# Late routed rows in 22 whole tiles and 5 tiles shared by two experts, with column-strip matmuls and a load for each half

## The reference, cut to what matters

```python
scores = softmax(x @ gate_w.T); topk_ids, topk_w = grouped_topk(scores)      # 2 experts for each row
combine = zeros((T, 8)).at[arange(T)[:, None], topk_ids].add(topk_w)
gu = einsum('th,eih->tei', x, w13_weight)            # w13: 8 x 1024 x 256
gate, up = gu[..., :512], gu[..., 512:]
act = silu(gate) * up * combine[:, :, None]
out = einsum('tei,ehi->th', act, w2_weight)          # w2: 8 x 256 x 512
x = x + out
```

## Time and profile before

| | |
|---|---|
| median of 3 runs | 552.11 us |
| span of the profiled execution, first to last instruction | 551.1 us |
| that execution's time with what lies around the span | not given; the median is 1.0 us above the span |
| busy: PE / PEld / DVE / ACT / POOL | 98 / 81 / 52 / 46 / 31% of the span |
| granted TensorE clock | 0.999 of full |
| moved by DMA | 74.30 MB, mean 135 GB/s |

### The profile page before, as it was taken

How to read it: one execution, slowest core, us unless ns; L and a number is a source line. 1 busy time by engine, 2 the same in 40 slices (tenths; PEclk the granted TensorE clock), 3 DMA queues, 4 the chain that set the end, 5 groups by cost and what they waited for, 6 DMA issues and landing times.

```text
span 551.1 us, 11061 instructions
## 1 busy us (share of the span) xinstructions
PE 538.4 (98%) x3967; PEld 444.4 (81%) x3968; DVE 284.0 (52%) x847; ACT 254.1 (46%) x587; POOL 168.7 (31%) x152
## 2 busy tenths in 40 slices
PE   9999999999999999999999889999999999999995
PEld 7887878777655676777777679999999999999995
DVE  4867676988562776855788865722212111212110
ACT  1343476263346767687787834542222222222221
POOL 2211000002145222332222043354335454445533
PEclk9999999999999999999999999999999999999999
DMA  8940000000110000300470657968788888898733
GB/s 320 403 141 1 2 0 2 0 1 2 38 39 0 2 2 1 116 1 2 135 287 7 227 172 244 318 187 268 221 246 219 248 229 236 239 255 238 239 66 38
DMA packets 28651, 74.30 MB, mean 135 GB/s; under 512 B 5600, under 2 KB 20320, under 8 KB 23360
## 3 DMA queue, kind: packets, MB, share of 16 engines
q1 hardware_dynamic: 18592, 61.87, 31.9%
q0 software_dynamic: 7488, 10.39, 10.6%
q10 hardware_dynamic: 2528, 1.48, 0.9%
HBM read 62.88 MB, written 10.85 MB: 134 GB/s over the span
## 4 chain that ended last, share of the span: by engine, by line
PE 93%; ACT 4%; DVE 1%; issue 1%; POOL 0%; DVEq 0%; POOLq 0%
PE ps L897 64%; PE ps L1193 12%; PE ps L901 11%; ACT ring L617 2%; PE ps L1041 1%; PE ps L1050 1%; ACT ring L624 1%; PE ps L1053 1%; PE ps L1044 1%; PE ps L981 1%; PE ps L1024 1%; ACT HF L629 0%; ACT ring L658 0%; POOL out_x L422 0%; PE ps L1122 0%
## 5 line engine op out<-in xcount | busy, mean ns | idle before, releaser
L897 PE MATMUL ps<-keep,arena 128*128 128x128 f32 (+2 forms) x976 | 114.9, 274 | 0.0
L897 PEld LDWEIGHTS ps<-keep,arena 128*128 128x128 f32 x976 | 112.8, 192 | 1.5 <-issue 1.1
L2014 DVE TENSOR_TENSOR keep<-keep,ps 128x512 f32<-128x512 f32 x39 | 26.8, 686 | 145.7 <-PE ps L897 124.2
L422 POOL DMA_INDIRECT out_x<-arena,row_no x38 | 59.9, 1576 | 102.1 <-DMA out_x<-arena,row_no 65.2
L1193 PE MATMUL ps<-arena,keep 128*128 x312 | 73.7, 380 | 0.1
L665 ACT COPY keep<-ps 128x256 f32<-128x256 f32 x39 | 14.5, 372 | 107.1 <-PE ps L901 103.8
L381 POOL TENSOR_TENSOR ring<-arena,keep 128x512 f32<-128x512 f32 x32 | 33.5, 1049 | 96.9 <-PE ps L897 79.8
L1193 PEld LDWEIGHTS ps<-arena,keep 128*128 128x128 f32 x312 | 56.4, 190 | 6.6 <-issue 0.3
L617 ACT ACTIVATE ring<-ps,mx 128x128 f32<-128x128 f32 x192 | 52.3, 403 | 6.2 <-DVE mx L1714 6.2
L897 PE MATMUL ps<-ring,arena 128*32 128x128 f32 (+1 forms) x640 | 53.1, 348 | 1.5 <-ACT ring L624 1.4
L373 POOL TENSOR_TENSOR var_x<-var_x,minus_half 128x4 f32<-128x4 f32 x16 | 16.5, 1036 | 115.8 <-DVE var_x L1570 115.8
(11 more groups left out here) (266 smaller groups left out, 816.2 us busy)
## 6 DMA issues: line engine op xcount, KB each, us to landing
arena<-in_w SPq DMA_DIRECT2D x29, 1024.0 KB
w_first<-in_w SPq DMA_DIRECT2D x10, 1024.0 KB
arena<-in_w SPq DMA_DIRECT2D x8, 512.0 KB, 7.3
keep<-in_keep SPq DMA_DIRECT2D x1, 3115.0 KB, 20.8
ring<-in_fold SPq DMA_DIRECT2D x1, 2112.0 KB, 12.7
arena<-in_x SPq DMA_DIRECT2D x4, 512.0 KB, 10.5
arena<-in_ctxT SPq DMA_DIRECT2D x4, 512.0 KB, 7.1
arena<-in_ctx SPq DMA_DIRECT2D x4, 384.0 KB, 11.2
```

Source lines behind the costliest of these rows:

```text
L422: pool.indirect_dma_start(out=out_d, out_offset=bass.IndirectOffsetOnAxis(ap=rows_at, axis=0), in_=YO[t % DEEP], in_offset=None, compute_o ...
L897: ins = pe.matmul(out, w, m, start=(k == 0), stop=(k == len(pairs) - 1))
L2014: dve.tensor_tensor(HA[r % 2], HA[r % 2], ps[:, 2 * (r % 2) + 1, :], ALU.mult).then_inc(act_ok, 1)
```

## The change

`NT` falls from 39 to 36: 9 early tiles, 22 late whole tiles of one expert, and 5 shared ones at t = 15, 19, 23, 27 and 31 (`SPLIT_AT`), each made of two halves of 64 pairs, which may belong to different experts. Expert by expert, full tiles (and rests above 64) go to whole tiles while there are any, the rest goes to halves.

A shared tile differs from a whole one at each station. SP loads two w13 (one for each half) into two buffers of their own, `W13_HALF`, in the arena. POOL gathers its 128 rows as before, but adds them by two DMAs of 64 rows, the second of which waits until the first has landed (a row can be in both halves). PE forms gate and up with the rows standing and the weights moving (`gate_up_halves`, 8 matmuls of 64 standing and 512 moving columns, the two halves in the two column strips of the array); the product then has the pairs on partitions, so it is turned by 4 transposes (`turn_act`) and copied by ACT (`act_turned`) before `down_halves` (8 matmuls of 64 x 256). ACT copies the two experts' w2 into `W2_HALF` three tiles ahead (two copies of 128 x 1024). The loops are written out, with no `Fori`.

On DVE the places of the whole tiles are found and published first (`late_tiles`, `late_hot(0, ...)`, `late_rows`), those of the halves after it (`late_halves`, `half_tiles`, `late_hot(1, ...)`, `half_rows`) between the steps of tiles 7 to 9, and PE has a second `place_late(1)`, again 32 small matmuls, ahead of tile 9's step.

```diff
-NT = B * S * NPICK // P + NE - 1
 EB = 2 * GB
 EARLY = -(-(EB * S * NPICK - NE * (P - 1)) // P)
-LATE = NT - EARLY
+HALF = P // 2
+LEFT = B * S * NPICK - EARLY * P
+HALVES = LEFT // HALF + NE - 1
+LATE = HALVES // 2 - NE // 2
+SHARED = -(-HALVES // 2) - LATE
+WHOLE, STRIPS, PLACES = EARLY + LATE, 2 * SHARED, LATE + 2 * SHARED
+NT = WHOLE + SHARED
+SPLIT_AT = tuple(NT - 5 - 4 * n for n in reversed(range(SHARED)))
...
+            def weights(c, to, landed):
+                e = sp.value_load(e_id[0:1, c:c + 1], min_val=0, max_val=NE - 1)
+                sp.dma_start(to, w13_d[bass.ds(e, 1), :, :].rearrange("e p n -> (e p) n")).then_inc(landed, 16)
+
+            def weights_of_half(n, h):
+                if n:
+                    sp.wait_ge((u_ps, y_ps)[h], SPLIT_AT[n - 1] + 1)
+                else:
+                    sp.wait_ge(e_known, 3)
+                    sp.wait_ge(stored[NG - 1], 32)
+                    sp.wait_ge(s["gl_ps"], NG)
+                    sp.wait_ge(s["ot_ps"], ALL)
+                weights(WHOLE + 2 * n + h, W13_HALF[h], half_in)
...
             sp.wait_ge(e_known, 1)
-            for t in range(NT):
-                if t == 1:
+            ran = [t for t in range(NT) if t not in SPLIT_AT]
+            for c, t in enumerate(ran):
+                if c == 1:
                     sp.wait_ge(s["ot_ps"], 2 * UNITS)
-                if t == 2:
+                if c == 2:
                     sp.wait_ge(s["ot_ps"], 3 * UNITS)
                     sp.wait_ge(xi_in[1], 16)
-                if t == 3:
+                if c == 3:
                     sp.wait_ge(stored[2], 32)
-                if t == EARLY:
+                if c == EARLY:
                     sp.wait_ge(e_known, 2)
-                if t >= DEEP:
-                    sp.wait_ge(u_ps, t - DEEP + 1)
-                e = sp.value_load(e_id[0:1, t:t + 1], min_val=0, max_val=NE - 1)
-                sp.dma_start(W13[t % DEEP], w13_d[bass.ds(e, 1), :, :].rearrange("e p n -> (e p) n")).then_inc(w13_in[t % DEEP], 16)
-            sp.wait_ge(added, 16 * NT)
+                if c >= DEEP:
+                    sp.wait_ge(u_ps, ran[c - DEEP] + 1)
+                weights(c, W13[c % DEEP], w13_in[c % DEEP])
+                for n in range(SHARED):
+                    for h in range(2):
+                        if t == SPLIT_AT[n] + (1 + h if n else 2 * h - 1):
+                            weights_of_half(n, h)
+            sp.wait_ge(added, 16 * adds_up_to(NT - 1))
...
+                    pool.wait_ge(added, 16 * adds_up_to(min(t, NT - 2) - 1))
+                c = column(t)
+                if t in SPLIT_AT:
+                    for n in range(2):
+                        own = slice(HALF * n, HALF * (n + 1))
+                        rows_at = row_upper[:, c - WHOLE:c - WHOLE + 1] if n else row_no[0:HALF, c:c + 1]
+                        if n:
+                            pool.wait_ge(added, 16 * (adds_up_to(t) - 1))
+                        pool.indirect_dma_start(out=out_d, out_offset=bass.IndirectOffsetOnAxis(ap=rows_at, axis=0),
+                                                in_=YO[t % DEEP][own, :], in_offset=None, compute_op=ALU.add).then_inc(added, 16)
+                    return
...
+            def w2_of_halves(n):
+
+                if n:
+                    act.wait_ge(y_ps, SPLIT_AT[n - 1] + 1)
+                else:
+                    act.wait_ge(e_known, 3)
+                    act.wait_ge(w2_in, 16 * NE)
+                    act.wait_ge(s["ot_ps"], ALL)
+                for h in range(2):
+                    c = WHOLE + 2 * n + h
+                    e = act.value_load(e_id[0:1, c:c + 1], min_val=0, max_val=NE - 1)
+                    act.copy(W2_HALF[h], w2e[:, bass.ds(e * W2_N, W2_N)]).then_inc(w2_half, 1)
+
+            def act_turned(r):
+                act.wait_ge(at_ps, split_up_to(r))
+                act.copy(HA[r % 2], bank(FEED)).then_inc(at_ok, 1)
+
+            def step(r):
+                turned(r + 2)
+                answer(r - 1)
+                if r in SPLIT_AT:
+                    act_turned(r)
+                gate(r + 1)
+                if r + 3 in SPLIT_AT:
+                    w2_of_halves(SPLIT_AT.index(r + 3))
...
+            def gate_up_halves(r):
+
+                pe.wait_ge(xt, r + 1)
+                pe.wait_ge(half_in, 32 * split_up_to(r))
+                for g in range(2):
+                    for k in range(KD):
+                        for h in range(2):
+                            own = slice(HALF * h, HALF * (h + 1))
+                            at = (2 * k + g) * INTER
+                            ins = pe.matmul(ps[own, 2 * (r % 2) + g, :], XIT[r % 2][:, k, own], W13_HALF[h][:, at:at + INTER], start=(k == 0), stop=(k == KD - 1))
+                    ins.then_inc((g_ps, u_ps)[g], 1)
+
+            def turn_act(r):
+                pe.wait_ge(act_ok, r + 1)
+                if r == SPLIT_AT[0]:
+                    pe.wait_ge(pair_known, 1)
+                    pe.wait_ge(routed, 3)
+                for i in range(INTER // P):
+                    ins = turn(bank(FEED)[:, i * P:(i + 1) * P], HA[r % 2][:, i * P:(i + 1) * P])
+                ins.then_inc(at_ps, 1)
+
+            def down_halves(r):
+                pe.wait_ge(at_ok, split_up_to(r))
+                pe.wait_ge(w2_half, 2 * split_up_to(r))
+                pe.wait_ge(y_ok, r - 1)
+                for i in range(INTER // P):
+                    for h in range(2):
+                        own = slice(HALF * h, HALF * (h + 1))
+                        ins = pe.matmul(Y_PS[r % 2][own, :], HA[r % 2][:, i * P + HALF * h:i * P + HALF * (h + 1)], W2_HALF[h][:, i * D:(i + 1) * D],
+                                        start=(i == 0), stop=(i == INTER // P - 1))
+                ins.then_inc(y_ps, 1)
+
+            def step(r):
+                turn_in(r + 2)
+                if r in SPLIT_AT:
+                    turn_act(r)
+                if r + 1 in SPLIT_AT:
+                    gate_up_halves(r + 1)
+                else:
+                    gate_up(r + 1)
+                if r in SPLIT_AT:
+                    down_halves(r)
+                else:
+                    down(r)
...
-            turn_pair()
-            tiles_of(pe, step)
-            gate_up(0, NT - 1)
-            down(0, NT - 2)
-            down(0, NT - 1)
+            gate_up(4, (0,))
+            gate_up(4, (1,))
+            turn_in(6)
+            down(3)
+            down(4)
+            gate_up(5, (0,))
+            gate_up(5, (1,))
+            gate_up(6, (0,))
+            place_late(0)
+            turn_in(7)
+            down(5)
+            gate_up(6, (1,))
+            gate_up(7, (0,))
+            turn_in(8)
+            down(6)
+            gate_up(7, (1,))
+            gate_up(8, (0,))
+            gate_up(8, (1,))
+            turn_in(9)
+            down(7)
+            gate_up(9, (0,))
+            gate_up(9, (1,))
+            turn_in(10)
+            down(8)
+
+            place_late(1)
+            for r in range(EARLY, NT - 2):
+                if r == EARLY + 1:
+                    turn_pair()
+                step(r)
+            gate_up(NT - 1)
+            down(NT - 2)
+            down(NT - 1)
...
             late_tiles()
-            late_hot()
-            gated(0, 5)
-            pick(0, 6)
+            late_hot(0, whole_at[:, :])
+            gated(5)
+            pick(6)
             late_rows()
             last_rows()
-            gated(0, 6)
-            pick(0, 7)
-            gated(0, 7)
-            pick(0, 8)
-            gated(0, 8)
-            pick(0, 9)
-            pick(0, 10)
-            gated(0, 9)
-            match_rows()
-            tiles_of(dve, step)
-            gated(0, NT - 1)
+            gated(6)
+            pick(7)
+            late_halves()
+            gated(7)
+            pick(8)
+            half_tiles()
+            gated(8)
+            pick(9)
+            late_hot(1, tile_at)
+            pick(10)
+            gated(9)
+            half_rows()
+            for r in range(EARLY, NT - 2):
+                step(r)
+                if r == EARLY + 1:
+                    match_rows()
+            gated(NT - 1)
             add_matched()
```

More of the change, by code:

```diff
@@ L268, in build, with split_up_to, column, adds_up_to @@
         XT_PS, Y_PS = ps[:, 4, 0:D], [ps[:, 5 + u, 0:D] for u in range(2)]
[L270 to L279 removed]
+        assert SPLIT_AT[0] > EARLY + 2
+        def split_up_to(r):
+            return sum(t <= r for t in SPLIT_AT)
+        def column(r):
+            return WHOLE + split_up_to(r) - 1 if r in SPLIT_AT else r - split_up_to(r)
+        def adds_up_to(r):
+            return r + 1 + split_up_to(r)
         def bank(k):
@@ L1504, in _ @@
             hidden1(15)
-            turn_in(0, 0)
-            turn_in(0, 1)
-            gate_up(0, 0, (0,))
+            turn_in(0)
+            turn_in(1)
+            gate_up(0, (0,))
             outputs1(15)
-            gate_up(0, 0, (1,))
```

(28 more changed lines are left out.)

396 lines of the change are left out of this document (227 added, 169 removed).

## The result

| | before | after |
|---|---|---|
| time, median (lowest to highest) | 551.93 us (551.71 to 552.84) | 570.08 us (563.59 to 572.95, 4 runs) |
| ratio after / before | | 1.028 (95%: 1.024 to 1.032) |
| profiled execution: time, span | | 563.59, 560.6 us |
| add(15) starts, add(NT-2) starts | 429.82, 544.83 us | 432.16, 554.38 us |

Forecast were 549.9 us and a range of 543 to 560. The change makes the kernel 2.8% slower.

The account below looks back on a forecast made before the run. The adds' chain, not PE, was to bound the end: PE gains 9.7 us, but add(NT-2) moves only from 544.83 to 542.6; with 6.3 us behind it and 1.0 beyond the span, 549.9 us, range 543 to 560.

Parts of the forecast that it names:

- The adds and not PE set the end: End of the kernel: last add due at 542.6 us by the adds, PE's answer ready at 533.9; chance 0.37.
- the free rounds: Adds after the last weight load, start to start: 4.57 us for a whole add, 3.6 us for a half.
- the tail of 6.3 us: Time behind the start of add(NT-2) to the end of the span, taken to stay at 6.3 us.
- DVE's longer list: Placing the halves on DVE: half_tiles 5.1 us, pushing gated(8) to 378.4 us, still early enough for PE; cost nothing.
- no tile waits for weights: 41 loads in place of 39 were to arrive in time, the second half's load issued 13 us ahead of use.
- PE's part: PE alone: -16.56 us for three tiles, +5.95 for five shared ones at +1.19 each, +0.91 for place_late(1): -9.7 us.
- the term for an add beside loads: Adds' chain in the shared stage: 9 whole rounds at 5.5 us, 49.5, and 8 halves at 4.1 us, 32.8.
- It fits: DMA time of three whole tiles and a shared one: 21.5 us within PE's 23.3, a share of 0.92 after 0.84.
- The lag: Delay of an add's start behind its tile's answer: growing to 8 to 9 us at tile 30.
- a stall does not lengthen the adds' chain: PE stalls on late gathers from a lag of about 9 us, which was taken not to lengthen the adds' chain.
- the second add: Rival: a half costs nearly a whole round, 5.2 us beside loads, 4.3 free; time near 562 us; chance 0.27.
- adds caught up by 0.15 us a tile: Reading of the kernel before, add(15) to add(33): adds' round trips 5.37 us each against PE's 5.52 a tile.

Follow-up runs that it names:

- a_paced: The changed kernel with each w13 load from the 13th on held until POOL's mark n-8 behind an add; nothing left out; 552.91 us, 1.001 of before.
- a_merged: The changed kernel with loads held for adds, and each shared tile added by one DMA after PE sums paired answers; full output; 547.56 us, 0.991 of before.
- a_single: The changed kernel with each shared tile added by one DMA of 128 rows, the upper half's answers going to blank rows; 553.65 us, 1.002 of before.
- b_two_adds: The kernel before, loops written out, with whole tiles 15, 19, 23, 27 and 31 added in two DMAs of 64 rows; 571.43 us, 1.032 of before.
- b_five_loads: The kernel before with five more w13 loads of 1 MB that nobody reads, each close behind a regular one; 567.21 us, 1.026 of before.

## Why the prediction was wrong

**Right.** The adds and not PE set the end (add(34) starts 6.6 us after its answer); the free rounds (half 3.6, measured 3.34 and 3.95; whole 4.57, measured 4.5), the half with some luck: its issue was put at 1.0 us and took 1.42, its landing at 2.3 and took 1.6 and 2.2; the tail of 6.3 us (6.2); DVE's longer list costs nothing; no tile waits for weights. PE's part was right in kind and too dear: 0.6 us a shared tile in place of 1.19.

**The step that failed** is the term for an add beside loads. I took the 0.8 us that before's rounds show on average over the free 4.57 as a property of "beside the loads", raised it to 5.5 for the denser ones, and halved it for halves. Measured in the same places of after: nine whole ones of 6.03 us on average, +4.8 us; eight halves of 4.74 in place of 4.1, +5.1; and add(15) starts 2.0 us later, behind rounds of 9.0 and 8.1 us at 391 and 400, where the first halves' loads follow on regular ones. 4.8 + 5.1 + 2.0 = 11.9, against the 11.8 by which add(NT-2) was late (554.38 for 542.6). The mechanism behind it, as the packets of the long rounds and a_paced show: before, loads came about one a tile, as the adds did; the change puts two or three close together, and an add is held by the one ahead and stretched by the one behind. "It fits" by a share of 0.92 was an average and told nothing of that; the share even fell.

**What followed from it.** The lag was forecast at 8 to 9 us by tile 30, with PE stalls only close. Whole adds start up to 15.0 us after their answers (tile 20), and the gather for t+6 stands behind add(t) in POOL's order, so PE stalls for 11.3 us; at tile 30 the lag is 7.8 us because PE itself is late by then. The sentence "a stall does not lengthen the adds' chain" held as far as waits go: from tile 10 on no add waits for its answer. Whether a stall shifts the loads onto other adds, and costs something by that, isn't shown.

The gains don't add up: the second adds taken away give 15 us, a load 9, spacing 16, spacing and merging 21. In part this may be because PE's own end is near: add(34) starts 6.6 us after its answer in after, 3.6 in a_paced, 1.8 in a_merged and 0.8 in a_single. The rest is open.

The rival "the second add" named 562 and its rule (over 4.4 us a half beside loads) held: 4.74. Its reason was half right: few rows queue behind the same weight packets, yes; but free halves are as short as forecast. It had too low a chance at 0.27, since I had read from before that adds caught up by 0.15 us a tile, and took that for room; b_two_adds shows that an added DMA makes the chain longer by its full 4.6 us there.

Open: the 568.7 us of after are 5 us over the profiled execution, and that one alone has a trace. Over the four executions the mean granted clock falls as the time grows (0.988, 0.985, 0.979 and 0.976 for 563.6, 568.7, 571.5 and 573.0 us), as longer stalls of PE would make it, but which comes first isn't shown. And by what order the packets of two queues are mixed, behind the first of them, isn't settled.

## What to carry to other kernels

When a chain of small dependent DMAs runs beside large loads, price a further link at its full round, and look at where the loads stand in time to the links, not at the share of DMA time: two loads in a row cost the link between them 7.6 us from the end of its issue to its landing in place of 2.7 here. A load with lead to spare is cheap to space (a mark behind each link, a wait before each load), and a gather that feeds the engine had better not hang on the same chain (PE lost 11.3 us to that here; no run takes it off the chain).

## What the runs showed of the hardware that was not expected

- An accumulating DMA of 64 rows takes 1.43 us of issue on POOL, one of 128 rows 1.57: halving the rows saves 0.14 us of issue. A gather of 128 rows takes 1.01.
- The first packet of an accumulating DMA comes 2.15 us after its start (64 rows: 2.0), but up to 4.3 us in after and 4.9 in b_five_loads where loads of 1 MB stand close together, and the next starts 1.2 us behind its last. Loads halved in bytes brought it down to 3.7. Loads cut into 2 KB packets made the changed kernel 7 us slower, not faster.
- Column strips of 64 at 512 moving columns run together in full: gate_up_halves, 16 matmuls as the profile counts, is 3.59 us, where a whole tile's gate_up with the whole array is 3.57.
